# A four-layer conditional kernel on one core: one program per engine, weight loads first, the first block's rows copied inside SBUF

## The reference

```
x = x + L0(x, length, ...)     # per channel h: causal convolution along t with kernel K[h], cut at length[b]
x = x + L1(x, cond, W)         # per sample: W[cond[b]] mixes the 64 channels (64 x 64)
x = x + L2(x, a, ...)          # x @ base_weight.T + bias + (x @ A[a[b]].T) @ B[a[b]].T     1024 -> 1024, rank 16
x = x + L3(x, l, ...)          # x @ W.T + 0.5 * (x @ A[l[b]]) @ B.T                        1024 -> 1024, rank 32
K[h] = 2 Re sum_n Cs[h,n] exp(dtA[h,n] t)     # 64 complex exponentials per channel
```

## Time and profile before

| | |
|---|---|
| median of 3 runs | 1456.32 us (1455.8 to 1456.84) |
| the profiled execution, its own time | 1456.79 us |
| its span in the trace | 1454.2 us |
| TensorE busy | 1425.4 us (98%) |
| VectorE, ScalarE, GpSimd busy | 1129.9, 611.8, 97.8 us |
| TensorE's granted clock, mean | 0.996 |

### The profile page before, as it was taken

One profiled execution on the slowest core, in us unless ns is written; L12 is line 12 of the kernel. 1 busy time (PEld: TensorE's weight loads), 2 busy tenths in 40 slices (PEclk: granted clock), 3 DMA queues, 4 the chain that ended last, 5 costly groups with the idle time before them and its releaser, 6 DMA issues.

```text
span 1454.2 us, 31508 instructions
## 1 busy us (share of the span) xinstructions
PE 1425.4 (98%) x9304; PEld 1325.1 (91%) x9304; DVE 1129.9 (78%) x2297; ACT 611.8 (42%) x1217; POOL 97.8 (7%) x184
## 2 busy tenths in 40 slices
PE   6999999999999996999999999999999999999998
PEld 5988899999999996989999999999999999999998
...
GB/s 312 0 131 75 59 288 273 274 273 272 280 269 274 275 232 209 132 170 199 149 163 204 147 167 199 145 161 204 152 153 196 171 152 184 185 152 164 203 153 80
DMA packets 116786, 271.94 MB, mean 187 GB/s; under 512 B 23881, under 2 KB 60109, under 8 KB 114097
## 3 DMA queue, kind: packets, MB, share of 16 engines
...
## 4 chain that ended last, share of the span: by engine, by line
PE 59%; DMA 1%; SPq 1%; DVE 1%; issue 0%; ACT 0%; DVEq 0%; ACTq 0%
PE ps L1599 18%; PE ps L1592 16%; PE ps L1591 12%; PE ps L1572 8%; PE ps L1608 4%; PE ps L1583 1%; PE ps L1578 1%; DMA out<-y_out 0%; DMA x_in<-x_d 0%; SPq L392 0%; SPq L1281 0%; SPq L1275 0%; DVE late L1444 0%; SPq L1287 0%; DVE x_in L1449 0%
## 5 line engine op out<-in xcount | busy, mean ns | idle before, releaser
L1591 PE MATMUL ps<-weights,xa 128*128 128x256 f32 x1152 | 322.0, 281 | 1.6 <-ACT y_out L1382 1.6
L1592 PE MATMUL ps<-weights,xa 128*128 128x352 f32 x1152 | 322.9, 322 | 0.0
L1599 PE MATMUL ps<-weights,xs 128*128 128x512 f32 x1152 | 291.3, 401 | 0.0
L1599 PEld LDWEIGHTS ps<-weights,xs 128*128 128x128 f32 x1152 | 207.1, 189 | 40.4
L1230 PE MATMUL ps<-toep,ut 128*128 128x512 f32 (+2 forms) x1152 | 226.7, 342 | 0.0
L1591 PEld LDWEIGHTS ps<-weights,xa 128*128 128x128 f32 x1152 | 217.4, 189 | 4.0 <-issue 2.6
L1592 PEld LDWEIGHTS ps<-weights,xa 128*128 128x128 f32 x1152 | 216.2, 188 | 1.3
L1230 PEld LDWEIGHTS ps<-toep,ut 128*128 128x128 f32 x1152 | 194.3, 189 | 16.6
L1358 ACT ACTIVATE a<-ps 128x512 f32<-128x512 f32 x128 | 76.4, 597 | 285.3 <-PE ps L1572 270.2
L1572 PE MATMUL ps<-m_gath,x_in 128*128 128x128 f32 x1024 | 137.1, 278 | 9.6 <-DVE x_in L1457 9.6
L1572 PEld LDWEIGHTS ps<-m_gath,x_in 128*128 128x128 f32 x1024 | 129.0, 194 | 12.3 <-DVE x_in L1457 9.8
...
## 6 DMA issues: line engine op xcount, KB each, us to landing
...
tab<-a_d SPq DMA_DIRECT2D x128, 128.0 KB, 2.1
stack<-b_d SPq DMA_DIRECT2D x126, 128.0 KB, 3.9
```

What stands on the lines that cost most here:

```text
L1591: mm(acc[:, left, 0:HALF], x_part, w[:, 0:HALF], start=start, stop=end, skip_group_check=True)
L1592: ins = mm(acc[:, right, 0:HALF + KR], x_part, w[:, HALF:WIDE], start=start, stop=end, skip_group_check=True)
L1599: ins = mm(acc[:, bank], operand[:, a, i, :], plain(i, b, m), start=opens and i == a == b == 0, stop=i == K4 - 1 and a == 1, skip_group_ch ...
```

## The change

It has two places.

**The start.** SyncE issues the first piece of L3, the first block of L2 and the second piece of L3 before the three small loads (`logs` twice, `aim`). VectorE does `triangle()` first and then the whole chain of exponentials; the low part of `d4`'s block is now the last step of `triangle()`, no longer GpSimd's. TensorE multiplies the identity by itself 20 times before the first real product (`keep_clock`; results are overwritten). `d0` asks for high and low parts one by one instead of for all at once, and `d4` runs pass by pass over all pieces, so that its first two passes need no low part of its block. `parameters()` stands after the fifth group instead of the fourth.

**The seam.** The two blocks become one program per engine (the functions `dense_sync`, `dense_gpsimd` and so on are the old second block, called at the end of the first list), so the engines no longer meet. SyncE loads channels 0 to 61 of the first two tiles when channel 61 is stored, in pieces of 60 and 2 rows; the rows of channels 62 and 63 are copied inside SBUF from `yo` to `x1_in` (`last_rows`, one 4 KB row each), those of the last channel on two queues, tile 0 by SyncE and tile 1 by ScalarE. The store of channel 63 comes after that. The index values of the first pair are read during the last group of convolutions. ScalarE's loads of the first pair's `stack` rows go to SyncE, behind the first `load_x1`. GpSimd clears `m_gath` and gathers while the last convolution runs, and takes over ten small fillings (`hrow`, `hc`, `hs`) from VectorE. TensorE multiplies the identity 12 times between the last convolution and the first quarter.

The diff, without the second block's functions that only moved:

```diff
 # SyncE, start
-            for to, of in ((logs[:, 0:N], log_a_real), (logs[:, N:N + 1], log_dt.unsqueeze(1)), (aim[:], a_imag)):
-                sp.dma_start(to, of).then_inc(in_small, 16)
             for i in range(K8):
                 sp.dma_start(w3_raw[:, i], w3[i]).then_inc(in_w3[i], 16)
                 if i == 0:
                     load_p2(p2[0], 0, in_w2[0])
+                if i == 1:
+                    for to, of in ((logs[:, 0:N], log_a_real), (logs[:, N:N + 1], log_dt.unsqueeze(1)), (aim[:], a_imag)):
+                        sp.dma_start(to, of).then_inc(in_small, 16)
 # GpSimd, start
             for i in BLOCKS[1:]:
                 p2_identity(p2[i], i, in_w2[i])
-                if i == 1:
-                    pool.wait_ge(staged_lo, 1)
-                    stage_low(1)
+            pool.wait_ge(staged_lo, 2)
 # VectorE, start
                     w3_identity(i + 1)
                 p3_low(i)
+            dve.wait_ge(staged_hi, 2)
+            tt(staged[1][:, 1], p2[4][:], f(staged[1][:, 0]), ALU.subtract).then_inc(staged_lo, 1)
...
+            triangle()
             dve.wait_ge(in_small, 16 * SMALL)
-            exp_parts(logs[:], e_k[:], e_f[:], e_q[:], e_2k[:], e_i[:], between=triangle)
+            exp_parts(logs[:], e_k[:], e_f[:], e_q[:], e_2k[:], e_i[:])
 # TensorE, start
+            pe.wait_ge(consts, 2)
+            keep_clock(target("a3a"), FILL_START)          # 20 matmuls ident x ident
             for c in range(K8):
-                pe.wait_ge(p3_lo, c + 1)
-                pe.wait_ge(staged_lo, 1)
-                ins = chunk_of(target("d0"), 0, c)
+                for a, b in ((0, 0), (1, 0), (0, 1)):
+                    pe.wait_ge((p3_hi, p3_lo)[b], c + 1)
+                    pe.wait_ge((staged_hi, staged_lo)[a], 1)
+                    for half in range(2):
+                        cols = slice(half * HB, (half + 1) * HB)
+                        ins = mm(target("d0")[:, cols], staged[0][:, a, c, :], p3[:, c, b, cols], ...)
...
-            split_job("d4")
+            job("d4")
+            for a, b in ((0, 0), (0, 1), (1, 0)):
+                pe.wait_ge((staged_hi, staged_lo)[a], 2)
+                for c in range(K8):
+                    for half in range(2):
+                        cols = slice(half * HB, (half + 1) * HB)
+                        ins = mm(target("d4")[:, cols], staged[1][:, a, c, :], p3[:, c, b, cols], ...)
...
-                    if i == 3:
+                    if i == 4:
                         parameters()
 # SyncE, seam (last group of channels)
             for u in range(UNROLL - 3):
                 channel(GROUPS - 1, u, loads=False)
+                if u < 4:
+                    first_ids.append(ids(sp, 0, u % 2, (1 + u // 2) * B))
...
-            sp.wait_ge(conv_done, C - 3)
             for v in range(2):
                 sp.dma_start(x_nat[v][:], x_rows[v]).then_inc(x_landed[v], 16)
-            channel(GROUPS - 1, UNROLL - 2, loads=False)
-            channel(GROUPS - 1, UNROLL - 1, loads=False)
             for u in range(2):
-                sp.wait_ge(x1_stored[u], count_in(GROUPS, 0, 2))
+                sp.wait_ge(x1_stored[u], stored_all - 16)
             for v in range(2):
-                sp.dma_start(x1_in[v][:], x1_rows[v]).then_inc(x1_landed[v], 16)
+                if v == 1:
+                    sp.wait_ge(conv_done, C - 1)
+                for b in range(2):
+                    for first, end in ((0, EVEN_ROWS), (EVEN_ROWS, C - 2)):
+                        sp.dma_start(x1_in[v][b * C + first:b * C + end], x1_d[2 * v + b, first:end]).then_inc(x1_landed[v], 16)
+            sp.wait_ge(y_front, C - 1)
+            sp.wait_ge(y_back, C - 1)
+            for v in range(2):
+                last_rows(sp, C - 2, v, row_landed)
+            store_y(GROUPS - 1, UNROLL - 2)
+            sp.wait_ge(y_front, C)
+            sp.wait_ge(y_back, C)
+            last_rows(sp, C - 1, 0, x1_landed[0])
+            dense_sync(sp)
...
 # new
+    def last_rows(eng, c, v, landed):
+        for b in range(2):
+            row = b * C + c
+            eng.dma_start(x1_in[v][row:row + 1], yo[c % 2][2 * v + b:2 * v + b + 1]).then_inc(landed, 16)
 # SyncE, head of the second part
-            a, l = [ids(sp, 0, v, B) for v in range(2)], [ids(sp, 0, v, 2 * B) for v in range(2)]
+        sp.dma_start(x1_d[:, C - 1], yo[(C - 1) % 2][:]).then_inc(x1_stored[1], 16)
+        sp.wait_ge(conv_done, C)
             (six loads of constant rows of stack, as before)
-            sp.wait_ge(c_fixed, 2)
-            for v in range(2):
-                load_c(v, a[v], l[v])
             for v in range(2):
                 sp.wait_ge(chosen[v], 2)
                 sp.dma_start(x_nat[v][:], x_rows[2 + v]).then_inc(x_landed[v], 16)
+        sp.wait_ge(c_fixed, 2)
+        for v in range(2):
+            load_c(v, a[v], l[v])
+        for u in range(2):
+            sp.wait_ge(x1_stored[u], stored_all)
             def stacks(n):
                 if isinstance(n, int) and n == 0:
+                    for v in range(2):
+                        load_stack(sp, v, first_ids[v])
                     return
 # ScalarE, end of the convolutions and head of the second part
+            act.wait_ge(y_front, C)
+            act.wait_ge(y_back, C)
+            last_rows(act, C - 1, 1, x1_landed[1])
...
-            for v in range(2):
-                load_stack(act, v, ids(act, 0, v, B))
+        act.wait_ge(x1_stored[0], stored_all)
+        act.wait_ge(row_landed, 64)
 # GpSimd: clears m_gath and gathers after pool.wait_ge(toep_lo, C), in the first part; then
+        pool.wait_ge(x1_stored[1], stored_all)
+        for v in range(2):
+            pool.wait_ge(x1_landed[v], LANDED_FIRST)
             (c_gath as before, then the ten fillings of hrow, hc, hs, each awaited; small_fixed)
 # VectorE, between sums(0) and the first pair
-            (the same ten fillings)
+        dve.wait_ge(small_fixed, 10)
+        dve.wait_ge(x1_stored[1], stored_all)
 # TensorE, head of the second part
+        keep_clock(acc[:, S_LEFT], FILL_BETWEEN)           # 12 matmuls ident x ident
         for q in range(4):
             quarter(0, q, FIRST_BANKS[q])
```

735 lines of the change are left out of this document (375 added, 360 removed).

## The result

The changed kernel takes 1444.4 us (median of 6 runs, 1442.2 to 1445.8), the kernel before 1456.4 (6 runs, 1455.3 to 1457.4): a ratio of 0.9917, 95% interval 0.9904 to 0.9930. That is 12.0 us less, where 13.5 were forecast. The profiled execution took 1442.18, the fastest of the six.

A forecast was written before the change was run, and what follows sets the result against it. TensorE's own work was taken to bound the kernel, apart from waits at the start and the seam. Gains of 4.0 and 9.5 us, 13.5 together, took 1456.79 to 1443.3, as median 1442.9 us; range 1440.5 to 1449.5.

The forecast's parts named there:

- 4.0 at the start: Start: TensorE reaches `b2_0` at 50.0 instead of 54.17, 4.2 us gained, taken as 4.0; bounds 2.0 to 5.4.
- 9.5 at the seam: Seam: 5.4 for the row copies, 2.4 for the quarters, 1.7 for first-pair waits; bounds 5.8 to 10.5 us.
- Loads: Start: first block issued 1.9 us earlier, landing at 7.1 instead of 9.01; all of `triangle()` moves by 1.9 us.
- First and second product: Start: `d0` ends at 20.0; `d4` follows without a gap and ends at 31.0 instead of 36.47, 5.5 us gained.
- Exponentials, parameters: Start: VectorE's chain begins at 20.7 and ends at 43.0, only 1.0 us earlier than before; `b2_0` near 50.0.
- the wait of 1.2 us: Start: TensorE, after five groups at 41.8, waits for the parameters until 43.0.
- the price named: Start: the new order makes VectorE late; its chain ends 1.0 us earlier while TensorE comes 5.5 us earlier.
- The 0.3 us at `b2_2`: Behind the start: TensorE at 72.0, target freed by VectorE at 71.9; no wait or a few tenths.
- The clock at the start: Start: `d0` lost 2.5 us to the lower clock; 20 filling matmuls take this loss into TensorE's idle time.
- Seam: Row copies put the first choice at 552.9 instead of 558.34 (5.4 us); quarters at full clock take 3.6 (2.4 us).
- First pair: First pair behind the seam: all 2.4 us of TensorE's waits (1.6 and 0.8) go, 1.7 of them counted.
- rival (a): SyncE's list bounds the first pair: 2.4 us of waits stay, row copies take 3.5 us; 1446.0 us, chance 0.17.

The follow-up runs named there:

- seam_only: The changed kernel with the whole start put back as before and the seam kept as changed: 1445.1 us, ratio 0.9925 to the kernel before.
- both_late: The changed kernel with the small loads (and the store to `kern_d`) issued behind the large ones on SyncE and ScalarE: 1442.4 us, ratio 0.9912.
- par_early: The changed kernel with `parameters()` after four groups instead of five: 1447.1 us, ratio 0.9941 to the kernel before.
- low_pool: The changed kernel with the low part of `d4`'s block given back to GpSimd: 1445.6 us, ratio 0.9925 to the kernel before.
- start_0: The changed kernel without the 20 filling matmuls at the start: 1444.8 us, ratio 0.9927 to the kernel before.
- between_0: The changed kernel without the 12 filling matmuls between the last convolution and the first quarter: 1446.5 us, ratio 0.9939 to the kernel before.
- rows_dram: The changed kernel with the last channel's four rows stored to DRAM and loaded back instead of copied in SBUF: 1448.0 us, ratio 0.9951.

## Why the prediction was right, and where it wasn't

The time is in the range, 1.5 us above the forecast; the two profiled spans differ by 13.8 us, where the forecast's sum was 13.5. The split of that sum, 4.0 at the start and 9.5 at the seam, is borne out less well. By the medians the seam alone gives 10.6 us (seam_only), and the start adds 1.2 us or nothing (0.9917 and 0.9928 against 0.9925). The mechanism of the seam was right and its size a little too small; of the start the mechanism was right up to `b2_0`, and most of the gain is not seen in the time. That the two errors cancel is luck.

- **Loads.** The block lands at 5.7, not at 7.1: its way is 4.4 us, not the 5.7 that it had behind three small loads. But "all of `triangle()` moves by 1.9 us" was wrong: it moved by 0.7. I put the small loads behind piece 1 and didn't ask what they delay there. both_late shows it: piece 1, piece 2 and ScalarE's table, 1.9 us together, which is more than the 1.2 that were missing.
- **First and second product.** `d0` ends at 21.6 (forecast 20.0), `d4` at 32.5 (31.0), for that same reason; `d4` follows without a gap in 11.04, as said.
- **Exponentials, parameters.** The chain ends at 43.38 (43.0). It began 1.3 us later than forecast (22.04 against 20.7), but its part behind the first exponential's thirteen steps, put at 18.55, took 17.4 (25.96 to 43.38): GpSimd's second subtraction held a VectorE step up for 1.70 us there instead of 2.28, and other steps less. TensorE, 1.5 us later than forecast, arrives just then, and the wait of 1.2 us isn't there. `b2_0` at 50.34 (50.0). So the late loads, the shorter chain and the missing wait cancelled; the good number here is partly luck. par_early and low_pool confirm the price named: a wait, and the lock. The 0.3 us at `b2_2` were forecast as a few tenths.
- **The clock at the start.** The first trace agrees with "the filling takes the loss into idle time", and start_0 gives 1.7 us for it at `b2_0`, though nothing in the median. What the prediction left out is the new wait in `d0`, 1.0 to 2.0 us between its first two matmuls and the rest, behind which the clock fell in four of eight traces with this start; this takes 1.3 us of the start's 3.8. Counting matmuls instead of trusting the column was right (start_0).
- **Seam.** 5.4 forecast for the row copies, 5.5 measured; 2.4 for the quarters, 2.4 measured (of these 1.6 by the fillings, by between_0; the rest is the shorter gap's); M1 3.6 us behind the first quarter, 3.60 measured. rows_dram corrects what the 5.4 are: 2.1 for the copy in SBUF, 3.4 for the rest of the tiles being loaded ahead.
- **First pair.** 1.7 counted of 2.4. The 2.4 were misread from rows 2: only 1.14 + 0.79 = 1.9 us of it lay in the first pair, the last 0.41 two pairs later. In after they are gone from the first pair (0.3 to 0.6 stay in three other traces), but in nine of thirteen traces a wait of 0.7 to 1.7 stands in the second pair, where before had 0.5. A stretched table issue goes with it each time. That is a piece of rival (a), in pair 1 instead of at the turn: the forecast said that the tables of pair 1 had "about as much slack" as before; the slack was not enough for a stretched issue.
- **Median against trace.** The forecast carries a gain worked out for one profiled execution over to the median, and allows nothing for what differs between executions. The profiled one of after had neither the lost clock (1.3 us at `b2_0`) nor the wait behind a long table issue (0.7 to 1.7) and is 2.2 us below its median, 0.7 below the forecast. That the two make up the difference is likely and not shown: the other five executions weren't traced.

Not tried: the ten small fillings back on VectorE, `d4` in its old order with all else new, and the late small loads on one queue at a time.
